# Columns' t2 as a unit-matrix matmul in steps 0 to 69 of the first image pair, and a new place in PSUM for the columns' n, u and input part

## The chip, the cores and the metric

The kernel runs on one core of one Trainium2 chip. The metric is the device time of one execution in microseconds. Engines are named as in the profile: PE is TensorE, DVE is VectorE, ACT is ScalarE, POOL is GpSimd, SP is SyncE, which issues most DMAs.

## What is computed

Eight images of 192 channels and 128 x 128 pixels are group-normalized. Each goes through four scans of a gated recurrent unit, along the rows in both directions and along the columns in both directions. The four results are averaged and added to the input.

```python
def step(h, xg):                       # xg = seq @ W_ih.T + b_ih, seq = x @ Wi.T + bi
    hg = h @ W_hh.T + b_hh
    r = sigmoid(xr + hr)
    z = sigmoid(xz + hz)
    n = tanh(xn + r * hn)
    return (1.0 - z) * n + z * h       # 64 wide, 128 steps
out = hs @ Wo.T + bo                   # back to 192 channels
x + (right + down + left + up) / 4.0
```

## The kernel before, in words

**Tiling.** Images are worked on in four pairs, g = 0 to 3. The two images of a pair fill the two halves of the 128 partitions with 64 hidden channels each. Two recurrences run side by side in each of the 128 steps t of a pair: c = 0 is the rows' scan, c = 1 the columns' scan. Each has 256 columns, two directions of 128 sequences.

**One step.** For each c there is this chain. PE adds the state part of gate r to the input part that it computed earlier (`h_r` after `x_r`), ACT makes r (`gate_r`), and DVE makes t1 = (hn + bias) * r (`make_t1`, line 994) and t2 = t1 + xn (`make_t2`, line 999). ACT makes n = tanh(t2) (`gate_n`, line 670), DVE u = (z - 1) * n (`make_u`, line 1004) and h = v - u (`make_h`, line 1013), where POOL has made v = z * h (`make_v`). The new h starts the next step's `h_r`. Each engine has one order for both chains. ACT: r rows, z rows, r columns, n rows, z columns, n columns. DVE: t1 rows, t2 rows, t1 columns, u rows, t2 columns, h rows, u columns, h columns, with other work at fixed places between them.

**PE and its quarters.** A product of 64 x 64 weights with 256 columns of fp32 is one matmul in the program and shows as two MATMUL rows, two passes, in the trace. The state parts (`h_part`, lines 860 and 861) work from each half of the partitions into the same half. The input parts (`x_part`, lines 840 and 842) work from each half into the other half. They use different quarters of the array and run beside each other. In a step PE's order is: h_r rows, x_r columns, h_n rows, x_n columns, h_z rows, x_z columns, h_r columns, h_n columns, then x_r, h_z columns, x_n and x_z, where these x parts are the rows' for step t + 1.

**Other work in the steps.** For pairs 1 to 3, the previous pair's output is finished in 96 units. The first 63 (in steps 3 to 65) each have two matmul pairs that fetch x (`unit_x_half`, lines 806 and 808, `beside_state` in `scan`) around h_n of the columns, two output products later (`unit_half`), and ACT's `add_bias`. The other units, in steps 73 to 124, have only the output products, and DVE adds x (`add_x`, line 1025). In pairs 0 to 2, steps 71 to 126 project the next pair's input in 32 tiles. A tile has two halves in quarters of the input parts around h_n of the columns (`project_high`, lines 756 and 758), two in quarters of the state parts (`project_straight`), and two again in quarters of the input parts (`project_crossed`, lines 781 and 783). The crossed ones stand in the next step around h_n of the columns, or, in eight steps of a pair, at the end of the same step; ACT then copies the tile out (`project_next`, line 650). In steps 0 to 63 of pairs 0 to 2 DVE also takes statistics for the next pair (line 986).

**PSUM.** `rx_ps` (bank 0 rows, bank 3 columns) holds r's input and, in its second half, xn. `hn_ps` (bank 1, bank 4) holds hn, then n, and u in its second half. `z_ps` (bank 2, bank 5) uses its first half only.

Of the kernel before, what the change touches and what calls it, by code (L numbers as in the profile page):

```python
# [5 lines left out]
def gru_scan_2d_kernel(nc: bass.Bass, x, wi_t, bi, w_ih_t, w_hh_t, b_ih, b_hh, wo_t, bo,  # L6
# [24 lines left out]
    T = WW  # L31
# [98 lines left out]
    with ctx:  # L130
# [73 lines left out]
        rx_ps = [bank[0], bank[3]]  # L204
        hn_ps = [bank[1], bank[4]]
        z_ps = [bank[2], bank[5]]
        fin_ps = [bank[0:3], bank[3:6]]
        proj_ps = bank[6:8]
        next_ps = bank[6]
# [56 lines left out]

        NSD = 16
        NSP = 3

        def state_before(g, t):  # L270

            return (T + 1) * g + t + 1
# [318 lines left out]
        def _(act):  # L591
# [75 lines left out]

            def gate_n(g, t, c):
                act.wait_ge(t2_ready[c], T * g + t + 1)
                act.activation(hn_ps[c][:, 0:N2], r[:, c, :], ACT.Tanh, bias=bih[:, 2:3]).then_inc(n_ready[c], 1)  # L670

            def scan(g):
                for t in range(T):
# [32 lines left out]
        def _(pe):  # L706
# [130 lines left out]
            def x_part(ps, gate, c, t, start):  # L837

                px = pair_of(seq, c, t)
                pe.matmul(as_pair(ps[LOW, :], c), wx[HIGH, gate, :], px[HIGH], start=start, stop=False,  # L840
                          skip_group_check=True)
                return pe.matmul(as_pair(ps[HIGH, :], c), wx[LOW, gate, :], px[LOW], start=start, stop=False,  # L842
                                 skip_group_check=True)

            def x_z(g, t, c):
                if T * g + t > 0:
                    pe.wait_ge(z_ready[c], T * g + t)
                x_part(z_ps[c][:, 0:N2], 1, c, t, True).then_inc(x_z_ready[c], 1)

            def x_r(g, t, c):  # L850
                if T * g + t > 0:
                    pe.wait_ge(t2_ready[c], T * g + t)
                x_part(rx_ps[c][:, 0:N2], 0, c, t, True)

            def x_n(g, t, c):
                x_part(rx_ps[c][:, N2:2 * N2], 2, c, t, False).then_inc(x_rn_ready[c], 1)

            def h_part(ps, gate, t, c, start):
                state = h[:, c, (t + 1) % 2, :]
# [8 lines left out]
                h_part(rx_ps[c], 0, t, c, False).then_inc(pre_r[c], 1)  # L868

            def h_n(g, t, c):  # L870
                h_part(hn_ps[c], 2, t, c, True).then_inc(pre_n[c], 1)

            def h_z(g, t, c):
                pe.wait_ge(x_z_ready[c], T * g + t + 1)
# [2 lines left out]
            def scan(g):  # L877
                if g == 0:
                    pe.wait_ge(seq_written, TILES)
                    pe.wait_ge(ident_loaded, 32)  # L880
                else:
                    pe.wait_ge(seq_fetched, 16 * PIECES * g)
                    for i in (1, 2):
                        pe.wait_ge(border_fetched[i], 16 * g)
                x_r(g, 0, 0)
                x_n(g, 0, 0)
                x_z(g, 0, 0)
                for t in range(T):
                    u = unit_at[t] if g > 0 and t in unit_at else None
                    m = project_at[t] if g + 1 < PAIRS and t in project_at else None  # L890

                    ends = project_ends[t] if g + 1 < PAIRS and t in project_ends and m is None else None
                    beside_state = u is not None and u < N_ACT
                    beside_input = u is not None and m is None

                    h_r(g, t, 0)
                    if g > 0 and t == 0:
                        for i in (0, 3):
                            pe.wait_ge(border_fetched[i], 16 * g)
                    x_r(g, t, 1)  # L900
                    h_n(g, t, 0)
                    x_n(g, t, 1)
                    h_z(g, t, 0)
                    x_z(g, t, 1)

                    h_r(g, t, 1)
                    if m is not None:
                        project_high(g + 1, m, 0)
                    if ends is not None:
                        project_crossed(g + 1, ends, 0)  # L910
                    if beside_state:
                        unit_x_half(g, u, 0)
                    h_n(g, t, 1)
                    if m is not None:
                        project_high(g + 1, m, 1)
                    if ends is not None:
                        project_crossed(g + 1, ends, 1)
                    if beside_state:
                        unit_x_half(g, u, 1)
                    if t + 1 < T:  # L920
                        x_r(g, t + 1, 0)
                    h_z(g, t, 1)
                    if t + 1 < T:
                        x_n(g, t + 1, 0)
                    if m is not None:
                        project_straight(g + 1, m, 0)
                    if beside_input:
                        unit_half(g, u, 0)
                    if t + 1 < T:
                        x_z(g, t + 1, 0)  # L930
                    if m is not None:
                        project_straight(g + 1, m, 1)
                    if beside_input:
                        unit_half(g, u, 1)
                    if u is not None and not beside_input:
                        for side in range(2):
                            unit_half(g, u, side)
                    if m is not None and t in project_ends:
                        for side in range(2):
                            project_crossed(g + 1, m, side)  # L940
                    if g + 1 < PAIRS:
                        if t == S_MEANS:
                            group_means(g + 1)
                        if t == S_CHANNELS:
                            channel_stats(g + 1)
                        if t == S_BIAS:
                            mean_bias(g + 1)
# [25 lines left out]
        def _(dve):  # L973
# [22 lines left out]

            def make_t2(g, t, c):
                dve.wait_ge(t1_ready[c], T * g + t + 1)
                dve.tensor_tensor(r[:, c, :], rx_ps[c][:, N2:2 * N2], r[:, c, :], ALU.add).then_inc(t2_ready[c], 1)  # L999

            def make_u(g, t, c):

                dve.wait_ge(n_ready[c], T * g + t + 1)
                dve.scalar_tensor_tensor(out=hn_ps[c][:, N2:2 * N2], in0=z[:, c, :], scalar=1.0, in1=hn_ps[c][:, 0:N2],  # L1004
                                         op0=ALU.subtract, op1=ALU.mult).then_inc(u_ready[c], 1)

            def make_h(g, t, c):
                k = T * g + t
                dve.wait_ge(u_ready[c], k + 1)
                dve.wait_ge(v_ready[c], k + 1)  # L1010
                if k >= 2:
                    dve.wait_ge(h_added[c], k - 1)
                dve.tensor_tensor(h[:, c, t % 2, :], v[:, c, :], hn_ps[c][:, N2:2 * N2], ALU.subtract)\  # L1013
                   .then_inc(h_ready[c], 1)

            def add_x(g, u, k):
# [13 lines left out]
            def scan(g):  # L1030
# [4 lines left out]
                for t in range(T):  # L1035
# [9 lines left out]
                        add_x(g, unit_at[t - 1], 1)  # L1045
                    make_t1(g, t, 1)
                    make_u(g, t, 0)
                    make_t2(g, t, 1)
                    make_h(g, t, 0)
                    if stats:  # L1050
                        half_chunk_stats(g + 1, t, 1)
# [171 lines left out]
```

## Time and profile before

| | before |
|---|---|
| median of 3 runs | 2473.11 us (2460.13 to 2480.77) |
| the profiled execution's own time | 2473.35 us |
| its span, first to last instruction | 2471.5 us |
| mean granted PE clock | 0.987 of full speed |
| busy share PE, DVE, ACT, POOL | 88%, 82%, 64%, 62% |
| line 840, 842, 860, 861: MATMUL rows each | 6144 of about 385 ns, pipelined, up to four at once |

All stretches of steps look alike, so one step of a kind shows its stage. In a timeline an instruction's end is its start plus its duration. A MATMUL row's end is modelled, so the starts are what is read from PE's rows.

### The profile page before, as it was taken

Reading aid. Unit: us, or ns where it says so; the run is one execution under the profiler, and the core shown is the slowest. Engines: PE = TensorE matmul, PEld = TensorE weight load, DVE = VectorE, ACT = ScalarE, POOL = GpSimd, SP = SyncE. Lnnn points to the kernel's source line nnn. Section 1 sums busy time; section 2 is a strip of 40 time slices with the busy share of each in tenths; the row PEclk is TensorE's granted clock in tenths of the full one; section 3 lists DMA queues with packets and bytes.
Section 4 is the critical chain, followed back from the end, with each engine's and each line's share of the span. In section 5 each row is a group of like instructions: output and inputs, shape, how many; then the busy total and the mean of one; then the engine's idle time right before and its main releaser. Section 6 shows DMA issues by size and latency. Waiting matters only on the chain.

```text
span 2471.5 us, 79952 instructions
## 1 busy us (share of the span) xinstructions
PE 2180.6 (88%) x31528; PEld 1412.0 (57%) x31528; DVE 2017.6 (82%) x4978; ACT 1569.6 (64%) x3390; POOL 1537.0 (62%) x2119
## 2 busy tenths in 40 slices
PE   0679999899979999999979999999979999999995
PEld 0345555566646666566546666565646666555574
DVE  7319999877769999887869999887867887888874
ACT  0126666677758887676657788676657888666600
POOL 2007777677767776666757677666766777777710
PEclk9999999999989999999999999999999999999998
DMA  9993332257789997789999998589986665334699
GB/s 353 292 229 102 97 98 72 87 148 217 235 241 245 249 247 188 184 220 271 302 280 237 237 253 209 156 223 272 307 261 170 155 148 133 74 96 95 157 328 372
DMA packets 325716, 509.19 MB, mean 206 GB/s; under 512 B 24928, under 2 KB 140000, under 8 KB 325344
## 3 DMA queue, kind: packets, MB, share of 16 engines
q1 hardware_dynamic: 307296, 478.23, 70.3%
q10 hardware_dynamic: 18048, 25.85, 3.0%
q8 instruction: 252, 4.13, 0.7%
q14 instruction: 120, 0.98, 0.1%
HBM read 352.98 MB, written 151.01 MB: 204 GB/s over the span
## 4 chain that ended last, share of the span: by engine, by line
DVE 33%; PE 31%; ACT 16%; issue 8%; DMA 6%; POOL 3%; SPq 1%; ACTq 0%; DVEq 0%; POOLq 0%
PE bank L860 19%; DVE r L994 12%; DVE r L999 11%; ACT r L662 7%; DVE h L1013 5%; ACT z L666 5%; DMA work<-x 4%; DVE bank L1004 3%; ACT bank L670 3%; PE bank L840 3%; PE bank L958 2%; PE bank L842 2%; ACT work L657 2%; PE bank L861 1%; DVE bn L986 1%
## 5 line engine op out<-in xcount | busy, mean ns | idle before, releaser
L860 PE MATMUL bank<-h,wh 64*64 64x256 f32 x6144 | 1496.5, 386 | 117.0 <-DVE h L1013 101.2
L840 PE MATMUL bank<-seq,wx 64*64 64x256 f32 x6144 | 1547.0, 384 | 32.4 <-DMA seq<-seq_next 22.1
L842 PE MATMUL bank<-seq,wx 64*64 64x256 f32 x6144 | 1547.7, 384 | 0.5 <-issue 0.5
L861 PE MATMUL bank<-h,wh 64*64 64x256 f32 x6144 | 1497.6, 386 | 0.4 <-issue 0.4
L546 POOL TENSOR_TENSOR v<-z,h 128x256 f32<-128x256 f32 x1024 | 747.6, 730 | 623.5 <-ACT z L666 597.8
L860 PEld LDWEIGHTS bank<-h,wh 64*64 64x64 f32 x6144 | 712.1, 133 | 584.2 <-DVE h L1013 416.7
L840 PEld LDWEIGHTS bank<-seq,wx 64*64 64x64 f32 x6144 | 753.9, 132 | 211.1 <-DVE r L999 105.8
L554 POOL TENSOR_TENSOR hsum<-hsum,h 128x256 f32<-128x256 f32 x1024 | 752.0, 734 | 128.7 <-DVE h L1013 109.4
L842 PEld LDWEIGHTS bank<-seq,wx 64*64 64x64 f32 x6144 | 751.3, 132 | 32.0 <-issue 3.1
L994 DVE SCALAR_TENSOR_TENSOR r<-bank,bhh,r 128x256 f32<-128x256 f32 x1024 | 490.1, 479 | 266.8 <-ACT r L662 230.2
L861 PEld LDWEIGHTS bank<-h,wh 64*64 64x64 f32 x6144 | 701.7, 133 | 1.0
L666 ACT ACTIVATE z<-bank,brz 128x256 f32<-128x256 f32 x1024 | 486.0, 475 | 312.0 <-PE bank L861 293.6
L662 ACT ACTIVATE r<-bank,brz 128x256 f32<-128x256 f32 x1024 | 485.7, 474 | 184.2 <-PE bank L861 183.9
L670 ACT ACTIVATE bank<-r,bih 128x256 f32<-128x256 f32 x1024 | 486.0, 475 | 115.3 <-DVE r L999 103.3
L1004 DVE SCALAR_TENSOR_TENSOR bank<-z,bank 128x256 f32<-128x256 f32 x1024 | 430.7, 421 | 68.2 <-ACT bank L670 67.5
L1013 DVE TENSOR_TENSOR h<-v,bank 128x256 f32<-128x256 f32 x1024 | 425.4, 415 | 24.8 <-issue 4.0
L999 DVE TENSOR_TENSOR r<-bank,r 128x256 f32<-128x256 f32 x1024 | 430.9, 421 | 17.7
L986 DVE BATCH_NORM_STATS2 bn<-work 128x6 f32<-128x384 f32 x384 | 211.8, 551 | 6.7 <-DMA work<-x 6.7
L824 PE MATMUL bank<-work,wo_a 64*64 64x256 f32 x768 | 205.3, 384 | 1.2 <-issue 1.2
L826 PE MATMUL bank<-work,wo_b 64*64 64x256 f32 x768 | 205.8, 385 | 0.0
L808 PE MATMUL bank<-work,ident 64*64 64x256 f32 x756 | 203.0, 389 | 0.0
L806 PE MATMUL bank<-work,ident 64*64 64x256 f32 x756 | 197.5, 381 | 0.0
(94 smaller groups left out, 2436.8 us busy)
## 6 DMA issues: line engine op xcount, KB each, us to landing
work<-x SPq DMA_DIRECT2D x384, 384.0 KB, 6.2
out<-work SPq DMA_DIRECT2D x192, 384.0 KB, 4.7
work<-x SPq DMA_DIRECT2D x143, 512.0 KB, 7.0
work<-x SPq DMA_DIRECT2D x286, 128.0 KB, 7.2
work<-x SPq DMA_DIRECT2D x32, 768.0 KB, 6.7
seq_next<-work SPq DMA_DIRECT2D x48, 512.0 KB, 6.9
work<-hsum_last SPq DMA_DIRECT2D x48, 512.0 KB, 7.1
seq<-x SPq DMA_DIRECT2D x17, 512.0 KB, 7.1
```

The lines of the kernel that those rows point to most:

```text
L546: pool.tensor_tensor(v[:, c, :], z[:, c, :], h[:, c, (t + 1) % 2, :], ALU.mult).then_inc(v_ready[c], 1)
L554: pool.tensor_tensor(px, px, as_pair(h[:, c, t % 2, :], c), ALU.add).then_inc(h_added[c], 1)
L662: act.activation(r[:, c, :], rx_ps[c][:, 0:N2], ACT.Sigmoid, bias=brz[:, 0:1]).then_inc(r_ready[c], 1)
L666: act.activation(z[:, c, :], z_ps[c][:, 0:N2], ACT.Sigmoid, bias=brz[:, 1:2]).then_inc(z_ready[c], 1)
L670: act.activation(hn_ps[c][:, 0:N2], r[:, c, :], ACT.Tanh, bias=bih[:, 2:3]).then_inc(n_ready[c], 1)
L840: pe.matmul(as_pair(ps[LOW, :], c), wx[HIGH, gate, :], px[HIGH], start=start, stop=False, skip_group_check=True)
L842: return pe.matmul(as_pair(ps[HIGH, :], c), wx[LOW, gate, :], px[LOW], start=start, stop=False, skip_group_check=True)
L860: pe.matmul(ps[LOW, 0:N2], wh[LOW, gate, :], state[LOW], start=start, stop=True, skip_group_check=True)
L861: return pe.matmul(ps[HIGH, 0:N2], wh[HIGH, gate, :], state[HIGH], start=start, stop=True, skip_group_check=True)
L994: dve.scalar_tensor_tensor(out=r[:, c, :], in0=hn_ps[c][:, 0:N2], scalar=bhh[:, 2:3], in1=r[:, c, :], op0=ALU.add, op1=ALU.mult).then_inc( ...
L999: dve.tensor_tensor(r[:, c, :], rx_ps[c][:, N2:2 * N2], r[:, c, :], ALU.add).then_inc(t2_ready[c], 1)
L1013: dve.tensor_tensor(h[:, c, t % 2, :], v[:, c, :], hn_ps[c][:, N2:2 * N2], ALU.subtract)\
```

## The change

In the columns' chain, n and u move into the free second half of `z_ps` (bank 5), and the input part of n moves from the second half of `rx_ps` (bank 3) into the second half of `hn_ps` (bank 4), beside the state part of n. The waits follow. The columns' x_z now waits for the columns' h as well, and so stands behind h_r of the columns and not ahead of it; x_n of the columns waits for n of the step before; x_r of the columns waits for r and not for t2. This holds in all 512 steps. In steps 0 to 69 of pair 0, t2 of the columns is no DVE addition: PE adds t1 to xn in PSUM with a 64 x 64 unit matrix (`add_t1`, in the quarters of the state parts), and n reads PSUM.

```diff
+        xn_ps = [rx_ps[0][:, N2:2 * N2], hn_ps[1][:, N2:2 * N2]]
+        n_ps = [hn_ps[0][:, 0:N2], z_ps[1][:, N2:2 * N2]]
+        u_ps = [hn_ps[0][:, N2:2 * N2], z_ps[1][:, N2:2 * N2]]
...
+        def t2_on_pe(g, t):
+            return g == 0 and t < PROJECT_FROM - 1
...
             def gate_n(g, t, c):
                 act.wait_ge(t2_ready[c], T * g + t + 1)
-                act.activation(hn_ps[c][:, 0:N2], r[:, c, :], ACT.Tanh, bias=bih[:, 2:3]).then_inc(n_ready[c], 1)
+                before = xn_ps[1] if c == 1 and t2_on_pe(g, t) else r[:, c, :]
+                act.activation(n_ps[c], before, ACT.Tanh, bias=bih[:, 2:3]).then_inc(n_ready[c], 1)
...
             def x_z(g, t, c):
                 if T * g + t > 0:
                     pe.wait_ge(z_ready[c], T * g + t)
+                if c == 1 and t > 0:
+                    pe.wait_ge(h_ready[1], state_before(g, t))
...
             def x_r(g, t, c):
                 if T * g + t > 0:
-                    pe.wait_ge(t2_ready[c], T * g + t)
+                    pe.wait_ge(t2_ready[0] if c == 0 else r_ready[1], T * g + t)
...
             def x_n(g, t, c):
-                x_part(rx_ps[c][:, N2:2 * N2], 2, c, t, False).then_inc(x_rn_ready[c], 1)
+                if c == 1 and T * g + t > 0:
+                    pe.wait_ge(n_ready[1], T * g + t)
+                x_part(xn_ps[c], 2, c, t, c == 1).then_inc(x_rn_ready[c], 1)
...
+            def add_t1(g, t):
+                pe.wait_ge(t1_ready[1], T * g + t + 1)
+                pe.matmul(xn_ps[1][LOW], ident[LOW, :], r[LOW, 1, :], start=False, stop=True, skip_group_check=True)
+                pe.matmul(xn_ps[1][HIGH], ident[HIGH, :], r[HIGH, 1, :], start=False, stop=True,
+                          skip_group_check=True).then_inc(t2_ready[1], 1)
...
                     h_z(g, t, 0)
+
+                    h_r(g, t, 1)
                     x_z(g, t, 1)
-
-                    h_r(g, t, 1)
...
+                    if t2_on_pe(g, t):
+                        add_t1(g, t)
                     if t + 1 < T:
                         x_z(g, t + 1, 0)
...
-                    make_t2(g, t, 1)
+                    if not t2_on_pe(g, t):
+                        make_t2(g, t, 1)
```

The first place is PE's order in a step with a unit (pair 2, before): bank 2 is h_z of the rows, bank 5 x_z of the columns and later their h_z, bank 3 h_r, bank 4 h_n, and bank 7 the two halves that fetch x.

```order
L860 MATMUL bank2<-h,wh 64x256 [waits x_z_ready0]
L861 MATMUL bank2<-h,wh 64x256
L840 MATMUL bank5<-seq,wx 64x256 [waits z_ready1]
L842 MATMUL bank5<-seq,wx 64x256
L860 MATMUL bank3<-h,wh 64x256 [waits x_rn_ready1,h_ready1]
L861 MATMUL bank3<-h,wh 64x256
L806 MATMUL bank7<-work,ident 64x4x64 [waits unit_finished,xf_loaded2,unit_added,hs_loaded0]
L808 MATMUL bank7<-work,ident 64x4x64
L860 MATMUL bank4<-h,wh 64x256
L861 MATMUL bank4<-h,wh 64x256
L806 MATMUL bank7<-work,ident 64x4x64 [waits xf_loaded2]
L808 MATMUL bank7<-work,ident 64x4x64
```

The same place in the changed program:

```order
L872 MATMUL bank2<-h,wh 64x256 [waits x_z_ready0]
L873 MATMUL bank2<-h,wh 64x256
L872 MATMUL bank3<-h,wh 64x256 [waits x_rn_ready1,h_ready1]
L873 MATMUL bank3<-h,wh 64x256
L848 MATMUL bank5<-seq,wx 64x256 [waits h_ready1,z_ready1]
L850 MATMUL bank5<-seq,wx 64x256
L814 MATMUL bank7<-work,ident 64x4x64 [waits unit_finished,xf_loaded2,unit_added,hs_loaded0]
L816 MATMUL bank7<-work,ident 64x4x64
L872 MATMUL bank4<-h,wh 64x256
L873 MATMUL bank4<-h,wh 64x256
L814 MATMUL bank7<-work,ident 64x4x64 [waits xf_loaded2]
L816 MATMUL bank7<-work,ident 64x4x64
```

The input part x_z moved from ahead of h_r (bank 3) to behind it, between h_r and the first fetch of x, and it has two waits where it had one.

The second place is the end of a step of pair 0 on PE, before. Bank 5 is h_z of the columns; banks 0 and 2 are x_n and x_z of the rows for the next step, then its h_r.

```order
L860 MATMUL bank5<-h,wh 64x256 [waits x_z_ready1]
L861 MATMUL bank5<-h,wh 64x256
L840 MATMUL bank0<-seq,wx 64x256
L842 MATMUL bank0<-seq,wx 64x256
L840 MATMUL bank2<-seq,wx 64x256 [waits z_ready0]
L842 MATMUL bank2<-seq,wx 64x256
L860 MATMUL bank0<-h,wh 64x256 [waits x_rn_ready0,h_ready0]
```

The same place in the changed program:

```order
L872 MATMUL bank5<-h,wh 64x256 [waits x_z_ready1]
L873 MATMUL bank5<-h,wh 64x256
L848 MATMUL bank0<-seq,wx 64x256
L850 MATMUL bank0<-seq,wx 64x256
L888 MATMUL bank4<-r,ident 64x256 [waits t1_ready1]
L889 MATMUL bank4<-r,ident 64x256
L848 MATMUL bank2<-seq,wx 64x256 [waits z_ready0]
L850 MATMUL bank2<-seq,wx 64x256
L872 MATMUL bank0<-h,wh 64x256 [waits x_rn_ready0,h_ready0]
```

The unit-matrix pair into bank 4 came in between x_n and x_z of the rows, with its wait for t1.

The third place is DVE's order in a step of pair 0, before, from t1 of the columns (994) over u of the rows (1004), t2 of the columns (999) and h of the rows (1013) to h of the columns.

```order
L994 SCALAR_TENSOR_TENSOR r<-bank,bhh,r 128x256 [waits pre_n1,r_ready1]
L1004 SCALAR_TENSOR_TENSOR bank<-z,bank 128x256 [waits n_ready0]
L999 TENSOR_TENSOR r<-bank,r 128x256 [waits t1_ready1]
L1013 TENSOR_TENSOR h<-v,bank 128x256 [waits h_added0,v_ready0,u_ready0]
L986 BN_STATS bn<-work 128x6
L1004 SCALAR_TENSOR_TENSOR bank<-z,bank 128x256 [waits n_ready1]
L1013 TENSOR_TENSOR h<-v,bank 128x256 [waits h_added1,v_ready1,u_ready1]
```

The same place in the changed program:

```order
L1015 SCALAR_TENSOR_TENSOR r<-bank,bhh,r 128x256 [waits pre_n1,r_ready1]
L1025 SCALAR_TENSOR_TENSOR bank<-z,bank 128x256 [waits n_ready0]
L1034 TENSOR_TENSOR h<-v,bank 128x256 [waits h_added0,v_ready0,u_ready0]
L1007 BN_STATS bn<-work 128x6
L1025 SCALAR_TENSOR_TENSOR bank<-z,bank 128x256 [waits n_ready1]
L1034 TENSOR_TENSOR h<-v,bank 128x256 [waits h_added1,v_ready1,u_ready1]
```

The addition between u and h of the rows is gone from DVE.

## Rows read from the trace of the kernel before

**Rows 1.** The page: engines, and the chain that ended last by engine.
```profile
PE 2180.6 (88%) x31528; PEld 1412.0 (57%) x31528; DVE 2017.6 (82%) x4978; ACT 1569.6 (64%) x3390; POOL 1537.0 (62%) x2119
...
DVE 33%; PE 31%; ACT 16%; issue 8%; DMA 6%; POOL 3%; SPq 1%; ACTq 0%; DVEq 0%; POOLq 0%
```

**Rows 2.** Timeline of DVE, pair 0 step 43: start, duration, engine, line, operation.
```profile
348.58 0.41 DVE L1013 TENSOR_TENSOR h<-v,bank 128x256 f32<-128x256 f32 x1
...
349.38 0.41 DVE L1004 SCALAR_TENSOR_TENSOR bank<-z,bank 128x256 f32<-128x256 f32 x1
349.83 0.42 DVE L1013 TENSOR_TENSOR h<-v,bank 128x256 f32<-128x256 f32 x1
350.25 0.48 DVE L994 SCALAR_TENSOR_TENSOR r<-bank,bhh,r 128x256 f32<-128x256 f32 x1
...
351.58 0.47 DVE L994 SCALAR_TENSOR_TENSOR r<-bank,bhh,r 128x256 f32<-128x256 f32 x1
351.97 0.42 DVE L1004 SCALAR_TENSOR_TENSOR bank<-z,bank 128x256 f32<-128x256 f32 x1
352.29 0.42 DVE L999 TENSOR_TENSOR r<-bank,r 128x256 f32<-128x256 f32 x1
352.63 0.41 DVE L1013 TENSOR_TENSOR h<-v,bank 128x256 f32<-128x256 f32 x1
```

**Rows 3.** Timeline of ACT, the same step.
```profile
349.74 0.47 ACT L662 ACTIVATE r<-bank,brz 128x256 f32<-128x256 f32 x1 [0.56 <-PE bank L861]
...
351.04 0.47 ACT L662 ACTIVATE r<-bank,brz 128x256 f32<-128x256 f32 x1
351.41 0.47 ACT L670 ACTIVATE bank<-r,bih 128x256 f32<-128x256 f32 x1
```

**Rows 4.** Timeline of PE, the same step: h_r of rows (first pass), of columns (second).
```profile
349.05 0.43 PE L860 MATMUL bank<-h,wh 64*64 64x256 f32 x1 [0.32 <-DVE h L1013]
...
350.62 0.38 PE L861 MATMUL bank<-h,wh 64*64 64x256 f32 x1
```

**Rows 5.** Timeline of PE, pair 1 step 32, a unit's fetches of x.
```profile
851.22 0.40 PE L806 MATMUL bank<-work,ident 64*64 64x256 f32 x1
...
851.50 0.38 PE L808 MATMUL bank<-work,ident 64*64 64x256 f32 x1
...
851.93 0.38 PE L808 MATMUL bank<-work,ident 64*64 64x256 f32 x1
```

**Rows 6.** Timeline of DVE, pair 1 step 32.
```profile
849.33 0.41 DVE L1013 TENSOR_TENSOR h<-v,bank 128x256 f32<-128x256 f32 x1
...
852.33 0.47 DVE L994 SCALAR_TENSOR_TENSOR r<-bank,bhh,r 128x256 f32<-128x256 f32 x1
...
853.38 0.41 DVE L1013 TENSOR_TENSOR h<-v,bank 128x256 f32<-128x256 f32 x1
```

**Rows 7.** Timeline of PE, pair 3 step 32: second passes of h_z columns and x_r.
```profile
1967.74 0.38 PE L861 MATMUL bank<-h,wh 64*64 64x256 f32 x1
...
1967.93 0.37 PE L840 MATMUL bank<-seq,wx 64*64 64x256 f32 x1
```

**Rows 8.** Timeline of ACT, the same step: z of the columns.
```profile
1968.39 0.47 ACT L666 ACTIVATE z<-bank,brz 128x256 f32<-128x256 f32 x1 [0.30 <-PE bank L861]
```

**Rows 9.** Timeline of DVE, the same step: h of rows before, t1 of columns.
```profile
1964.78 0.41 DVE L1013 TENSOR_TENSOR h<-v,bank 128x256 f32<-128x256 f32 x1
...
1967.75 0.48 DVE L994 SCALAR_TENSOR_TENSOR r<-bank,bhh,r 128x256 f32<-128x256 f32 x1 [0.35 <-ACT r L662]
```

**Rows 10.** Timeline of PE, pair 1 step 104: h_n of the columns, second pass.
```profile
1159.58 0.38 PE L861 MATMUL bank<-h,wh 64*64 64x256 f32 x1
```

**Rows 11.** Timeline of DVE, the same step: t1 of the columns, which waits for PE.
```profile
1160.08 0.48 DVE L994 SCALAR_TENSOR_TENSOR r<-bank,bhh,r 128x256 f32<-128x256 f32 x1 [3.30 <-PE bank L861]
```

**Rows 12.** Timeline of ACT after pair 0 step 78, which projects a whole tile.
```profile
501.30 0.69 ACT L650 ACTIVATE work<-bank,bseq 128x512 f32<-128x512 f32 x1 [0.92 <-PE bank L783]
```

**Rows 13.** Groups by line and form: the halves of add_x on DVE.
```profile
L1025 DVE SCALAR_TENSOR_TENSOR work<-bank,bo_unit,work 128x256 f32<-128x256 f32 x132 | 62.8, 476 | 0.0
```

More of the change, by code:

```diff
@@ L870, in h_n @@
             def h_n(g, t, c):
-                h_part(hn_ps[c], 2, t, c, True).then_inc(pre_n[c], 1)
+                h_part(hn_ps[c], 2, t, c, c == 0).then_inc(pre_n[c], 1)
+            def add_t1(g, t):
[3 more added lines that the diff above has]
+                          skip_group_check=True).then_inc(t2_ready[1], 1)
             def h_z(g, t, c):
@@ L998, in make_t2 @@
                 dve.wait_ge(t1_ready[c], T * g + t + 1)
-                dve.tensor_tensor(r[:, c, :], rx_ps[c][:, N2:2 * N2], r[:, c, :], ALU.add).then_inc(t2_ready[c], 1)
+                dve.tensor_tensor(r[:, c, :], xn_ps[c], r[:, c, :], ALU.add).then_inc(t2_ready[c], 1)
             def make_u(g, t, c):
                 dve.wait_ge(n_ready[c], T * g + t + 1)
-                dve.scalar_tensor_tensor(out=hn_ps[c][:, N2:2 * N2], in0=z[:, c, :], scalar=1.0, in1=hn_ps[c][:, 0:N2],
+                dve.scalar_tensor_tensor(out=u_ps[c], in0=z[:, c, :], scalar=1.0, in1=n_ps[c],
                                          op0=ALU.subtract, op1=ALU.mult).then_inc(u_ready[c], 1)
@@ L1012, in make_h @@
                     dve.wait_ge(h_added[c], k - 1)
-                dve.tensor_tensor(h[:, c, t % 2, :], v[:, c, :], hn_ps[c][:, N2:2 * N2], ALU.subtract)\
+                dve.tensor_tensor(h[:, c, t % 2, :], v[:, c, :], u_ps[c], ALU.subtract)\
                    .then_inc(h_ready[c], 1)
```

## The prediction

> **What bounds the kernel now.** I read the page first. No engine is full: PE is busy for 88% of the span, DVE 82%, ACT 64%, and the chain that ended last changes between DVE, PE and ACT all the time [rows 1]. So a loop of dependences from step to step sets the pace, and the question is which one. The timelines of single steps show it.
>
> In pair 0 the rows' h of step 42 ends at 348.58 + 0.41 = 348.99 and that of step 43 at 352.63 + 0.41 = 353.04 [rows 2]: 4.05 us a step. The way between them: PE begins the rows' h_r 0.06 later, at 349.05, and runs without a gap to the columns' h_r, whose second pass begins at 350.62 [rows 4]. The columns' r starts at 351.04, 0.42 after that pass. ACT's order puts the rows' n behind it, at 351.41, 0.10 before r ends [rows 3]. DVE then works back to back: t1 of the columns at 351.58, u of the rows at 351.97, t2 of the columns at 352.29, h of the rows at 352.63 [rows 2]. Two things follow. The columns' t2 stands between u and h of the rows and costs the loop time. And each delay of the columns' t1 moves u, t2 and h of the rows one for one.
>
> With units the way is the same: in pair 1 the columns' t1 starts at 852.33 and the rows' h 1.05 later, at 853.38 [rows 6]. In pair 3, without statistics, t1 stands at 1967.75, 2.56 after the end of h at 1964.78 + 0.41 = 1965.19 [rows 9]; in pair 1 it is 852.33 - 849.74 = 2.59.
>
> **The DVE addition taken away, pair 0, steps 1 to 63.** Rows' loop: u ends at 352.39; a dependent h starts 0.04 later, as the columns' do (349.38 + 0.41 = 349.79, then 349.83) [rows 2]. So h would begin at 352.43 instead of 352.63 and end at 352.84, and this loop takes 4.05 - 0.20 = 3.85.
>
> Columns' loop, from the start of r: r 0.47; 0.04 to DVE (349.74 + 0.47 = 350.21, t1 of the rows at 350.25); t1 0.47; 0.06 to PE. The added pair of matmuls is two passes in each of two quarters, as h_r is. From the first pass of h_r (349.05) to ACT's r (349.74) it is 0.69 [rows 3, 4], which I take; n then starts 1.73 after r did. n takes 0.47, 0.04 and u 0.41, 0.04 and h 0.42, 0.06 and h_r 0.69 until the next r: 3.86. That is 0.01 above the rows' loop, so both are about as long, and the step takes 3.87. The gain is 0.18 x 63 = 11 us. Bounds: if the matmul costs no more than the DVE addition did, the rows' loop alone decides, 0.20 x 69 = 14 us; if it costs 0.18 more than 0.69, nothing is gained. For steps 64 to 69, which hold long statistics, I count nothing. PE's x_z of the rows stands behind add_t1's wait; it is needed only by h_z of the next step. ACT reading PSUM in n is priced at nothing: r, which reads PSUM, takes 0.47, as n does [rows 3].
>
> **x_z of the columns behind h_r, all steps.** In plain steps (pair 0 to step 70, pair 3 from step 66) the quarters of the input parts stand idle beside h_r and h_n of the columns, and the move is free: that idle slot is its cover. With a unit, or while a tile is projected, the cover is gone. The fetch of x began at 851.22, its second pass at 851.50 and the second fetch's at 851.93 [rows 5]. x_z now takes the first place, the first fetch the second, and so on: the first fetch's second pass begins at 851.93 instead of 851.50, one slot of 0.43 later.
>
> Who waits for that? h_n of the columns stands behind this fetch in the program. A row shows what that does. h_z of the columns stands behind x_r in the program; its second pass began first, at 1967.74, against 1967.93 for x_r's [rows 7]. Yet z started at 1968.39 [rows 8]: 0.65 after its own second pass, 0.46 after x_r's, where r needed 0.42. So matmuls in other quarters may start early, but their ends are reported in program order. h_n's end will then be reported behind the fetch's, and t1 waits for it. Where t1 waited for h_n alone, it began 1160.08 - 1159.58 = 0.50 after the second pass [rows 10, 11]; with the 0.04 by which z was late beyond r's 0.42 I take 0.53. So t1 begins at 851.93 + 0.53 = 852.46 instead of 852.33. Relative to the end of h that is 2.72, against 2.59 and 2.56 now.
>
> The Trainium skill, "TensorE: Matmul & The Clock Gate", section "What overlaps and what doesn't", says that matmuls start and end strictly in program order. The trace agrees on the ends and not on the starts. By the rule taken whole, h_n would also start behind the fetch, and the sum would be near 2670, by the rows 2517.
>
> DVE's back-to-back overlap with the statistics ahead of t1 goes too, so I take 0.145 a step in 122 steps with units and statistics (steps 3 to 63, pairs 1 and 2) and 0.16 in 65 without (63 of pair 3, step 64 of pairs 1 and 2): 18 + 10 = 28 us. Bounds: 0 if h_n's end is not held; 0.26 a step if x_z's second wait puts it 0.1 later than the fetch stands now.
>
> The three pairs that project have 56 such steps each, 168 in all, with a half tile between h_r and h_n. In 136 I take 0.16, 22 us. In 32 steps of pairs 1 and 2 a half of add_x, 0.476 [rows 13], already holds DVE up; between 0 and 0.16 I take 0.08, 2.5 us. Eight steps of a pair run a whole tile through as one serial chain, and ACT stood idle 0.92 for its end before copying it, with r of the rows behind [rows 12]. This chain is pushed by up to the slot of 0.43; I take 0.35, which is 0.2 more than counted: 24 x 0.2 = 5 us. Less some 2 us where PE waits for a tile's load anyway, this is 27.
>
> New waits: x_n of the columns waits for n of the step before. n ends about 0.2 after the rows' h, 0.4 in pair 0 with add_t1 (2.20 after r, against 352.84 - 351.04 = 1.80 for the rows' h); x_n's turn on PE comes 0.5 after h. I count nothing; if it were later by 0.1, what stands behind it (h_z of the rows, h_r of the columns) would move by as much. x_r's wait becomes earlier. No DMA is moved.
>
> **Sum.** 2473.35 (the profiled execution, 1.85 above its span, and 0.2 above the median of 2473.11) - 11 + 28 + 27 = 2517, 1.8% slower.
>
> **Rivals.**
> 1. Not slower: h_n's end isn't held by the fetch. This decides from one number, t1's start with units: at 2.6 after h or below, the 28 us and most of the 27 fall away. Only the serial tiles remain, 24 x 0.35 = 8 us, and with the 11 gained it is 2471. For it: the case seen is x_r and h_z [rows 7, 8], not fetch and h_n. Against it: the two cases have the same form.
> 2. Starts are held in program order too: another slot of 0.43 in 355 steps, 153 us, 2670. Against it: the starts [rows 7]. This is the rule of the Trainium skill, "TensorE: Matmul & The Clock Gate", named above.
> 3. The added matmul or x_z's dispatch costs more: no gain in pair 0, or 0.1 more in 355 steps; 2528 to 2555.
>
> The change does what it says: the order shows 70 additions gone and 70 pairs added.
>
> **How the numbers follow.** My forecast has a chance of 0.73, with a range of its own of 2497 to 2545. Rival 1 has 0.15 (2463 to 2480), rival 2 0.03, rival 3 beyond that range 0.06, and 0.03 is for a gain that I don't see. To hold 8 in 10 the range must reach rival 1's middle: 2470 to 2545. A measurement of this kernel tells about 1%, 25 us, from no change. Slower than 2498 is 0.80, within 1% 0.17, faster 0.03.
>
> **What would show it.** Right: in the profile after, pair 0's plain steps take 3.85 to 3.9; with units they take 4.19; t1 of the columns waits for PE in them, 0.5 after the fetch's second pass. Wrong: steps with units stay at 4.05, or pair 0's stay there too because n is late.

## The result, and the profile after

The changed kernel takes 2520.61 us (median of 4 runs, 2512.93 to 2524.03) against 2469.2 us for the kernel before (4 runs, 2460.13 to 2480.77, three of them those of the table ahead): a ratio of 1.0197, 95% interval 1.0171 to 1.0223. It is slower by about 2%; 2517 had been forecast.

The page of the changed kernel, its count of instructions, its engines and the chain that ended last by engine, stands against [rows 1]:

```profile
span 2511.1 us, 80950 instructions
...
PE 2294.4 (91%) x31808; PEld 1581.0 (63%) x31808; DVE 2018.3 (80%) x4908; ACT 1548.4 (62%) x3390; POOL 1533.5 (61%) x2119
...
PE 66%; DVE 12%; DMA 6%; ACT 5%; issue 5%; POOL 4%; ACTq 1%; SPq 0%; POOLq 0%; DVEq 0%
```

The chain now runs mainly through PE (66%, before 31%) and hardly through DVE (12%, before 33%). PE has only 280 more rows of 31528, so this isn't added work: the engines now wait for PE's ends where they waited for DVE's before.

**Pair 0, step 43.** Timeline of DVE after (h is line 1034, t1 1015, u 1025; compare [rows 2]):

```profile
338.52 0.42 DVE L1034 TENSOR_TENSOR h<-v,bank 128x256 f32<-128x256 f32 x1
...
341.53 0.48 DVE L1015 SCALAR_TENSOR_TENSOR r<-bank,bhh,r 128x256 f32<-128x256 f32 x1
341.93 0.42 DVE L1025 SCALAR_TENSOR_TENSOR bank<-z,bank 128x256 f32<-128x256 f32 x1
342.39 0.42 DVE L1034 TENSOR_TENSOR h<-v,bank 128x256 f32<-128x256 f32 x1
```

Between u and h nothing stands any more: h begins 0.46 us after u, where it was 0.66. From h to h it is 342.39 - 338.52 = 3.87 us; it was 4.05. The added matmuls on PE (lines 888 and 889), and n of the columns on ACT (line 678), which waits for them:

```profile
342.07 0.43 PE L888 MATMUL bank<-r,ident 64*64 64x256 f32 x1
...
342.35 0.38 PE L889 MATMUL bank<-r,ident 64*64 64x256 f32 x1
```

```profile
342.77 0.45 ACT L678 ACTIVATE bank<-bank,bih 128x256 f32<-128x256 f32 x1 [0.35 <-PE bank L889]
```

PE begins 0.06 after t1 ends (341.53 + 0.48 = 342.01) and ACT 0.70 after that.

**Pair 3, step 32, a step with a unit.** Timeline of PE after, columns: x_z (line 848), the first fetch (lines 816 and 814) and h_n (line 873). Two rows of one line here are its two passes.

```profile
2002.85 0.40 PE L848 MATMUL bank<-seq,wx 64*64 64x256 f32 x1
...
2003.31 0.38 PE L816 MATMUL bank<-work,ident 64*64 64x256 f32 x1
2003.34 0.38 PE L814 MATMUL bank<-work,ident 64*64 64x256 f32 x1
...
2003.43 0.38 PE L873 MATMUL bank<-h,wh 64*64 64x256 f32 x1
...
2003.56 0.38 PE L814 MATMUL bank<-work,ident 64*64 64x256 f32 x1
```

Timeline of DVE in the same step: h of the rows, t1 of the columns, the next h (compare [rows 9]):

```profile
2000.96 0.41 DVE L1034 TENSOR_TENSOR h<-v,bank 128x256 f32<-128x256 f32 x1
...
2004.10 0.48 DVE L1015 SCALAR_TENSOR_TENSOR r<-bank,bhh,r 128x256 f32<-128x256 f32 x1 [0.50 <-PE bank L873]
...
2005.16 0.41 DVE L1034 TENSOR_TENSOR h<-v,bank 128x256 f32<-128x256 f32 x1
```

h_n's second pass began at 2003.43. t1 began 0.67 later, but 0.54 after the fetch's second pass at 2003.56. Relative to the end of h (2000.96 + 0.41 = 2001.37), t1 stands at 2.73 instead of 2.56. The step takes 4.20.

**Where the time went.** I added up stretches of steps, from the end of one rows' h to that of a later one, in the profiled execution of each kernel; units are steps 0 to 64 of pairs 1 to 3, projection is steps 71 to 127 of pairs 0 to 2. Three more columns are experiments told of below.

| us | before | after | no second wait | both mended | pair 0 alone |
|---|---|---|---|---|---|
| pair 0, steps 0 to 64 | 258.96 | 247.46 | 247.32 | 247.27 | 247.28 |
| units | 789.79 | 818.59 | 798.96 | 791.59 | 791.05 |
| projection | 725.11 | 751.51 | 737.52 | 733.86 | 724.85 |

The change brings -11.5, +28.8 and +26.4. The sum is +43.7. The two profiled executions differ by 39.6, since the first h came 2.5 us earlier after, the end was 2.6 us shorter, and the other steps took 1.0 more. These parts vary from run to run (the first h came 172 to 181 us after the start in the ten profiled executions). The medians differ by 51.4, more than the stretches explain: the profiled execution of the changed kernel was the fastest of its four.

### The profile page after: what moved, and what is told of

The parts are those of the page before. It is cut to its first block, busy times and chain, and to the rows that moved or that the text cites. A ratio compares the mean times of both kernels' runs of the same rounds, so it can differ in the third digit from the quotient of the medians.

```text
span 2511.1 us, 80950 instructions
## 1 busy us (share of the span) xinstructions
PE 2294.4 (91%) x31808; PEld 1581.0 (63%) x31808; DVE 2018.3 (80%) x4908; ACT 1548.4 (62%) x3390; POOL 1533.5 (61%) x2119
## 3 DMA queue, kind: packets, MB, share of 16 engines
q8 instruction: 256, 4.19, 0.7%
## 4 chain that ended last, share of the span: by engine, by line
PE 66%; DVE 12%; DMA 6%; ACT 5%; issue 5%; POOL 4%; ACTq 1%; SPq 0%; POOLq 0%; DVEq 0%
PE bank L872 30%; PE bank L848 13%; PE bank L850 5%; DMA work<-x 4%; DVE r L1015 4%; PE bank L816 3%; PE bank L873 3%; PE bank L832 2%; ACT z L673 2%; DVE r L1020 2%; DVE bank L1025 2%; ACT r L669 2%; DVE h L1034 2%; PE bank L766 1%; POOL v L553 1%
## 5 line engine op out<-in xcount | busy, mean ns | idle before, releaser
L848 PE MATMUL bank<-seq,wx 64*64 64x256 f32 x6144 | 1631.0, 385 | 30.1 <-DMA seq<-seq_next 21.5
L850 PE MATMUL bank<-seq,wx 64*64 64x256 f32 x6144 | 1640.2, 387 | 0.0
L872 PE MATMUL bank<-h,wh 64*64 64x256 f32 x6144 | 1533.0, 386 | 49.7 <-DVE h L1034 36.1
L873 PE MATMUL bank<-h,wh 64*64 64x256 f32 x6144 | 1534.4, 386 | 1.2 <-issue 1.1
L872 PEld LDWEIGHTS bank<-h,wh 64*64 64x64 f32 x6144 | 703.1, 132 | 501.7 <-DVE h L1034 343.0
L848 PEld LDWEIGHTS bank<-seq,wx 64*64 64x64 f32 x6144 | 716.6, 132 | 155.2 <-DVE r L1020 52.5
L850 PEld LDWEIGHTS bank<-seq,wx 64*64 64x64 f32 x6144 | 716.7, 132 | 5.9 <-issue 1.0
L873 PEld LDWEIGHTS bank<-h,wh 64*64 64x64 f32 x6144 | 696.0, 132 | 6.5 <-issue 0.7
L678 ACT ACTIVATE bank<-r,bih 128x256 f32<-128x256 f32 x954 | 452.7, 475 | 39.5 <-DVE r L1020 38.4
L1020 DVE TENSOR_TENSOR r<-bank,r 128x256 f32<-128x256 f32 x954 | 402.2, 422 | 17.7
L816 PE MATMUL bank<-work,ident 64*64 64x256 f32 x756 | 193.5, 376 | 0.0
L814 PE MATMUL bank<-work,ident 64*64 64x256 f32 x756 | 193.4, 376 | 0.0
```

The source lines that it names most:

```text
L678: act.activation(n_ps[c], before, ACT.Tanh, bias=bih[:, 2:3]).then_inc(n_ready[c], 1)
L872: pe.matmul(ps[LOW, 0:N2], wh[LOW, gate, :], state[LOW], start=start, stop=True, skip_group_check=True)
L873: return pe.matmul(ps[HIGH, 0:N2], wh[HIGH, gate, :], state[HIGH], start=start, stop=True, skip_group_check=True)
```

## The experiments

My theory was that x_z behind h_r pushes the fetch, and that h_n's end, hence t1, is held behind the fetch because ends come in program order. The first rival was that the new PSUM places and waits cost the time. The second was that fuller quarters do, whatever the program order.

**h_n of the columns last, in the kernel before.** No quarter gets more work; only h_n's place in the program is later.

```diff
-                    h_n(g, t, 1)
                     if m is not None:
                         project_high(g + 1, m, 1)
                     if ends is not None:
                         project_crossed(g + 1, ends, 1)
                     if beside_state:
                         unit_x_half(g, u, 1)
+                    h_n(g, t, 1)
```

> The kernel before with h_n of the columns written behind both halves of the fetch (and of the half tiles), x_z and all else as before. No quarter gets more work and none gets its work in another order; only the place of h_n in the program is later. In the kernel before the second half of the fetch begins its second pass where the first half does in the changed kernel. If ends are held in program order, t1 of the columns begins about 2.72 us after the rows' h in steps with units although h_n itself runs as early as before, and about 0.16 us in each of 355 steps is lost: some 55 us, ratio 1.022. If ends are not held, h_n, which finds its quarters idle, ends as early as before, t1 stays at 2.59 and the ratio is 1.00.

Measured: 2525.98 us, ratio 1.0217 (1.0201 to 1.0233). Timeline of PE in pair 3, step 32: h_n's second pass (line 861), then the second fetch's (line 808). The timeline of DVE in that step stands below it: h of the rows and t1 of the columns.

```profile
2011.55 0.38 PE L861 MATMUL bank<-h,wh 64*64 64x256 f32 x1
...
2011.79 0.38 PE L808 MATMUL bank<-work,ident 64*64 64x256 f32 x1
```

```profile
2009.08 0.41 DVE L1013 TENSOR_TENSOR h<-v,bank 128x256 f32<-128x256 f32 x1
...
2012.34 0.48 DVE L994 SCALAR_TENSOR_TENSOR r<-bank,bhh,r 128x256 f32<-128x256 f32 x1 [0.64 <-PE bank L861]
```

h_n's second pass still begins 2011.55 - 2009.49 = 2.06 after h, as in all these kernels, yet t1 begins 0.79 after it and 0.55 after the second fetch's pass. The trace also has the moment at which h_n's semaphore was raised, relative to h (medians of steps 5 to 62): 2.46 in all pairs of the kernel before; here 2.63 in pair 1 and 2.74 in pairs 2 and 3, 0.45 behind the second fetch's second pass (2.18 and 2.30); in the changed kernel 2.63 in pairs 1 to 3, 0.44 behind the first fetch's (2.19). So h_n's end is held by what stands ahead of it in the program, with nothing else changed. That settles the mechanism. The total came out as expected, though not its parts: t1 stood at 2.74 with units in pair 1 and at 2.85 in pairs 2 and 3, where the fetch is later (see the next experiment), and the units lost 41 us, where they lose 29 in the changed kernel; the projection lost only 8, where it loses 26 there.

**x_z of the columns behind h_r, in the kernel before, and nothing else.**

```diff
                     h_z(g, t, 0)
-                    x_z(g, t, 1)
 
                     h_r(g, t, 1)
+                    x_z(g, t, 1)
```

> The kernel before with one line moved: x_z of the columns behind h_r of the columns, in all steps. No matmul is added, no PSUM place and no wait is changed; t2 of the columns stays on DVE everywhere. If the move itself is the cause (x_z takes the first place behind h_r, the fetch or the half tile moves one slot back, and the end of h_n is held behind it), t1 of the columns begins about 2.72 us after the rows' h ends in steps with units, against 2.59 before, these steps take about 4.19 instead of 4.05, and the run is about 55 us longer than before: some 2528, ratio 1.022. Pair 0 keeps 4.05 in its plain steps. If the new PSUM places and the waits that come with them are the cause, this kernel takes what before takes: ratio 1.00, t1 at 2.59.

Measured: 2488.87 us, ratio 1.0067 (1.0045 to 1.0089). Neither expectation held: some 17 us of the 55. In steps with units t1 stood at 2.617 after h, not at 2.73, and the steps took 4.09. x_z's first pass began 1.37 after h, not 1.48 as in the changed kernel. So in pair 1 the move itself puts the fetch's second pass back by 0.32 (in step 32 from 1.75 to 2.07 after h), not by 0.43. In the kernel before, with x_z elsewhere, the fetch began 1.48 after h in pair 1 (851.22 in [rows 5], h's end at 849.74). x_z alone can begin 0.11 earlier than that, but in the changed kernel it doesn't. The difference at x_z between the two kernels is a wait.

In pairs 2 and 3 the move costs the fetch only 0.21. Timeline of PE in the kernel before, pair 3 step 32 (h's end at 1965.19, [rows 9]): the first fetch's first and second pass, and h_n's second.

```profile
1966.78 0.40 PE L806 MATMUL bank<-work,ident 64*64 64x256 f32 x1
...
1967.06 0.38 PE L808 MATMUL bank<-work,ident 64*64 64x256 f32 x1
...
1967.25 0.38 PE L861 MATMUL bank<-h,wh 64*64 64x256 f32 x1
```

The fetch begins at 1.59 and not at 1.48, and its second pass at 1.86 (median) and not at 1.75. What the program has there in pairs 2 and 3 and not in pair 1 is one wait more ahead of the fetch, for `unit_finished`, which counts the units that DVE finished in the scans before and was fulfilled before this pair's scan began. No run takes this wait away, so that it is the cause is argued and not shown. With x_z ahead of the fetch this difference is gone: its second pass stands at 2.07 in all three pairs, and at 2.19 in the changed kernel.

**The changed kernel without that wait.** In it x_z of the columns waits for z and for h. h_r, ahead of it on the same queue, has waited for the same h, so the second wait is always fulfilled when it comes up.

```diff
             def x_z(g, t, c):
                 if T * g + t > 0:
                     pe.wait_ge(z_ready[c], T * g + t)
-                if c == 1 and t > 0:
-                    pe.wait_ge(h_ready[1], state_before(g, t))
```

> The changed kernel without the new wait of the columns' x_z on the columns' h of the step before; h_r of the columns, which now stands ahead of x_z on the same queue, waits for the same h, so the order of the data is unchanged. x_z stays behind h_r, all else stays. If this second wait is what makes the move dear (with it x_z's first pass began 1.48 us after the rows' h, without it, in the kernel with the move alone, 1.37), the fetch's second pass returns from 2.18 to 2.07, t1 of the columns from 2.73 to 2.62, steps with units from 4.20 to 4.10, and with the gain of 11.5 us in pair 0 the run takes about 11 us less than the kernel with the move alone: 2478, ratio to before 1.000 to 1.004. If the new PSUM places or the other new waits are the cause, t1 stays at 2.73 and the run at 2515 to 2520, ratio 1.02.

Measured: 2479.27 us (10 runs), ratio 1.0036 (1.0021 to 1.0051), as expected. The page counts 508 instructions fewer than that of the changed kernel, 4 x 127 steps:

```profile
span 2482.6 us, 80442 instructions
```

Timeline of PE in pair 3, step 32: x_z's first pass (line 848), h_n's second (line 871), the first fetch's second (line 814); below it DVE's h of the rows and t1 of the columns.

```profile
1975.37 0.43 PE L848 MATMUL bank<-seq,wx 64*64 64x256 f32 x1
...
1976.06 0.38 PE L871 MATMUL bank<-h,wh 64*64 64x256 f32 x1
1976.07 0.38 PE L814 MATMUL bank<-work,ident 64*64 64x256 f32 x1
```

```profile
1973.59 0.41 DVE L1032 TENSOR_TENSOR h<-v,bank 128x256 f32<-128x256 f32 x1
...
1976.62 0.48 DVE L1013 SCALAR_TENSOR_TENSOR r<-bank,bhh,r 128x256 f32<-128x256 f32 x1 [0.38 <-ACT r L669]
```

With h's end at 1974.00, x_z begins at 1.37 (it was 1.48) and the fetch's second pass at 2.07 (2.19), nearly together with h_n's at 2.06. t1 begins at 2.62 and is 0.55 behind the fetch again. A wait that never waits thus cost some 34 to 40 us, 19.6 + 14.0 by the table's stretches and (1.0197 - 1.0036) x 2470 = 40 by the ratios, as an instruction of its own on PE's queue ahead of a matmul on whose end others hang. It is the same 0.11 as at the fetch of pairs 2 and 3 in the kernel before. The new PSUM places and the other new waits are all still in this kernel, yet with units its t1 (2.62) and its period (4.09) are those of the kernel with the move alone, which has none of them: there they cost nothing. The Trainium skill, "Perfetto Trace Analysis", section "Identifying Dependency Chains", says that an instruction that waits on several engines may get separate semaphore instructions ahead of it for the further conditions; the count of 508 agrees.

**h_n ahead of the fetch, in the changed kernel.** x_z, its wait and the late fetch stay.

```diff
                     x_z(g, t, 1)
+                    h_n(g, t, 1)
                     if m is not None:
                         project_high(g + 1, m, 0)
...
                         unit_x_half(g, u, 0)
-                    h_n(g, t, 1)
```

> The changed kernel with h_n of the columns written ahead of the first half of the fetch, of the half tile and of the crossed tile; x_z of the columns stays behind h_r of the columns, so the fetch still begins one slot later. If a matmul's end is held behind the ends of what stands ahead of it in program order, h_n is free now: t1 of the columns returns to 2.56 to 2.62 us after the rows' h in steps with units, their period to 4.05, and the gain of 11 us in pair 0 remains: 2460 to 2480, ratio to before 0.995 to 1.003. What may stay are some microseconds of the tiles that run through in one step. If the full quarters (the slot itself, contention of input parts with state parts) are the cause, t1 stays at 2.72 and the run near 2517, ratio 1.02.

Measured: 2494.27 us, ratio 1.0084 (1.0063 to 1.0104), between the two expectations. In pair 3 the theory holds: t1 follows h_n, not the fetch. DVE in step 32, h of the rows and t1 of the columns, and PE's second pass of h_n (line 873):

```profile
1984.68 0.41 DVE L1034 TENSOR_TENSOR h<-v,bank 128x256 f32<-128x256 f32 x1
...
1987.65 0.48 DVE L1015 SCALAR_TENSOR_TENSOR r<-bank,bhh,r 128x256 f32<-128x256 f32 x1 [0.16 <-ACT r L669]
```

```profile
1987.15 0.38 PE L873 MATMUL bank<-h,wh 64*64 64x256 f32 x1
```

t1 stands at 2.56 after h, 0.50 behind h_n, and these steps take 4.03. In pairs 1 and 2 its median was 2.72 all the same. The timelines of ACT and DVE there (pair 1, the step behind the h at 901.77) show why: a unit's copy (line 664), r of the rows, then t1 and t2 of the rows, the statistics (line 1007), t1 of the columns.

```profile
902.50 0.69 ACT L664 ACTIVATE work<-bank,bo_high 128x512 f32<-128x512 f32 x1
903.08 0.47 ACT L669 ACTIVATE r<-bank,brz 128x256 f32<-128x256 f32 x1
```

```profile
901.77 0.41 DVE L1034 TENSOR_TENSOR h<-v,bank 128x256 f32<-128x256 f32 x1
...
903.58 0.48 DVE L1015 SCALAR_TENSOR_TENSOR r<-bank,bhh,r 128x256 f32<-128x256 f32 x1
904.10 0.42 DVE L1020 TENSOR_TENSOR r<-bank,r 128x256 f32<-128x256 f32 x1
904.44 0.55 DVE L1007 BATCH_NORM_STATS2 bn<-work 128x6 f32<-128x384 f32 x1
904.91 0.47 DVE L1015 SCALAR_TENSOR_TENSOR r<-bank,bhh,r 128x256 f32<-128x256 f32 x1
```

The late fetch pushes the rows' input parts that share its quarters, up to x_z, whose last pass on PE is this:

```profile
902.03 0.37 PE L850 MATMUL bank<-seq,wx 64*64 64x256 f32 x1
```

The second half of the unit's output products stands behind x_z in the program, and ACT's copy of the unit, which needs it, begins 0.47 after this pass. In step 32 of pair 1 that distance is 0.47 to 0.49 in this kernel, in the changed one and in the one without the second wait, where x_z comes earlier; in the kernel before it is 0.68, so there the copy waits for something else. The semaphores say the same (medians of pairs 1 to 3): the unit's is raised 0.06 after x_z's in every kernel, and the copy begins 0.02 after that in these three, 0.08 to 0.21 in the kernel before. Relative to h (901.77 + 0.41 = 902.18) the copy begins at 0.32 (median 0.30; 0.12 before) and r of the rows at 0.90 (0.75 before), and DVE runs back to back from there to t1 of the columns at 2.73. A late fetch has two ways to t1, and the longer one hid the other in the changed kernel. In pair 3, without statistics, DVE has room for it. Against the kernel before, the units lose 9.9 us here and the projection 20.0; in the projection t1 stood at 2.82 to 2.83 in pairs 1 and 2 (2.66 before), and what holds it there is not shown.

**Both mended:** the changed kernel without the second wait and with h_n ahead of the fetch.

> The changed kernel with both mended: no second wait at x_z of the columns, and h_n of the columns ahead of the fetch. If the end of h_n held behind the fetch and the late fetch (through ACT's copy of the unit, the rows' r, and DVE's order) are all there is, t1 stands at 2.56 in pair 3 and at 2.59 to 2.63 in steps with statistics, and the run is 3 to 12 us below the kernel without the second wait alone: 2464 to 2474, ratio 0.997 to 1.001. If h_n ahead of the fetch makes the fetch later and this costs as much as it saves, it equals the kernel without the second wait.

Measured: 2473.84 us (10 runs), ratio 1.0010 (0.9990 to 1.0029), the upper end of what was expected. t1 stands at 2.56 in pair 3 and at 2.63 to 2.64 in pairs 1 and 2 (2.59 to 2.63 expected). The steps with units cost 1.8 us more than before and the projection 8.8, about what pair 0 gains.

**The changed kernel with t2 on DVE everywhere.**

```diff
         def t2_on_pe(g, t):
 
-            return g == 0 and t < PROJECT_FROM - 1
+            return False
```

> The changed kernel without the added pair of matmuls: t2 of the columns is a DVE addition in all steps, also in steps 0 to 69 of the first pair; new PSUM places, waits and the place of x_z stay. If the added matmuls save what the first pair saves, its plain steps return to 4.05 us and the run is 11.5 us longer than the changed kernel: about 2532, ratio to before 1.024 to 1.025. If the new PSUM places alone shortened the first pair's steps, they stay at 3.87 and the run at 2520.

Measured: 2525.16 us, ratio 1.0213 (1.0197 to 1.0228), between the two expectations. The totals can't tell it from the changed kernel, their intervals overlap; the stretch can: pair 0's steps 0 to 64 took 258.97 us again, a step 4.05. So the added matmuls saved the 11.5 us, and not the new places, which also cost nothing there (258.96 before).

**The change in pair 0, steps 0 to 69, alone,** and the kernel before in all other steps.

```diff
+        def z_behind(g, t):
+            return t2_on_pe(g, t) or (t > 0 and t2_on_pe(g, t - 1))
...
-                    x_z(g, t, 1)
+                    if not z_behind(g, t):
+                        x_z(g, t, 1)
 
                     h_r(g, t, 1)
+                    if z_behind(g, t):
+                        x_z(g, t, 1)
```

> The change in pair 0, steps 0 to 69, alone: the new PSUM places, x_z of the columns behind h_r and t2 as matmuls in these steps only, everything as in the kernel before in all others. There the slot beside h_r and h_n of the columns is idle, so the gain of 11.5 us should remain and nothing be lost: 2458 to 2462 against 2471, ratio 0.9955, with pair 0's plain steps at 3.87 and steps with units at 4.05. If something else in the scan or its beginning lost time with the new places, the ratio is 1.00 or above.

Measured: 2459.88 us (12 runs), ratio 0.9958 (0.9943 to 0.9972). It beats both kernels, by the gain of pair 0 and nothing else (last column of the table).

**The same, and pair 3 from step 67 on too:**

```diff
-            return g == 0 and t < PROJECT_FROM - 1
+            return (g == 0 and t < PROJECT_FROM - 1) or (g == PAIRS - 1 and t > ACT_UNITS_UNTIL)
```

> As the kernel with the change in pair 0 alone, and the same in pair 3 from step 67 on, where no unit stands beside the columns' matmuls. 31 of these 61 steps hold nothing but the recurrence and took 4.13 us, 30 hold a unit on the input side and took 4.07. If DVE's addition between u and h of the rows costs the loop there what it cost in pair 0, 0.18 to 0.2 a step, 11 us more are gained: ratio 0.991. If what paces these steps is something else (their t1 stands at 2.66 instead of 2.56 in the plain ones), less than 4 us more: ratio 0.994 to 0.9955.

Measured: 2461.57 us (12 runs), ratio 0.9960 (0.9946 to 0.9975): no more gain, just above the second expectation. The steps divide otherwise than was written there: in the kernel before it is the 33 steps behind a unit that take 4.12, the others take 4.03 (medians). Timeline of PE from step 100 into 101 of pair 3: the added matmuls (line 900), the second half of a unit's output products (line 842), the next h_r of the rows (line 883); below it DVE's h of the rows from step 99 to 102.

```profile
2233.28 0.37 PE L900 MATMUL bank<-r,ident 64*64 64x256 f32 x1
...
2233.72 0.38 PE L842 MATMUL bank<-work,wo_c 64*64 64x256 f32 x1
...
2233.94 0.38 PE L842 MATMUL bank<-work,wo_c 64*64 64x256 f32 x1
...
2234.15 0.37 PE L883 MATMUL bank<-h,wh 64*64 64x256 f32 x1
```

```profile
2229.65 0.42 DVE L1049 TENSOR_TENSOR h<-v,bank 128x256 f32<-128x256 f32 x1
...
2233.51 0.42 DVE L1049 TENSOR_TENSOR h<-v,bank 128x256 f32<-128x256 f32 x1
...
2237.69 0.42 DVE L1049 TENSOR_TENSOR h<-v,bank 128x256 f32<-128x256 f32 x1
...
2241.98 0.42 DVE L1049 TENSOR_TENSOR h<-v,bank 128x256 f32<-128x256 f32 x1
```

Step 100 takes 3.86, as in pair 0. But the unit's second half stands behind the added matmuls and uses the same quarters, and h_r of the rows can begin only 0.22 after h (2233.93) instead of 0.06. Step 101 then takes 4.18 and step 102, behind a second unit in a row, 4.29; before, these three steps took 4.03, 4.11 and 4.12. Over steps 68 to 127 the 27 steps with no unit ahead gain 4.6 us and the 33 behind a unit lose 3.4. Over steps 71 to 127 pair 3 took 228.25 us, against 228.68 before.

## Why the prediction was right

- **DVE's addition gone from pair 0: held.** 3.867 a step over steps 1 to 63 (3.87 said), 11.5 us (11 said). From the added matmul's first pass to ACT it is 342.77 - 342.07 = 0.70, where 0.69 was taken from h_r and r. Steps 64 to 69, counted at nothing, brought nothing (+0.4 us over steps 64 to 71).
- **h_n's end held behind the fetch: held,** and shown alone by the kernel with h_n last. t1 at 2.729 (2.72 said), steps with units 4.20 (4.19 said), 28.8 us (28 said). That the 28 came out is in part luck: it was worked out from the fetch of pair 1 alone. In pairs 2 and 3 the fetch's second pass stood at 1.86 before; by the same rule, a slot of 0.43 and then 0.53, t1 would have gone to 2.82 there and the loss to 0.23 and 0.26 a step. It did not: behind x_z the fetch stands at the same place in all three pairs.
- **One slot of 0.43: the place was right, the reason for it only in part.** The fetch's second pass stands at 2.185 after h in all three pairs, where 851.93 - 849.74 = 2.19 was said; it moved by 0.43 in pair 1, but by 0.32 in pairs 2 and 3. But I took the whole 0.43 for x_z's two passes, because x_z would begin where the fetch had begun. Without its second wait it begins 0.11 earlier, since the quarters stand idle then, and the move costs 0.32 (0.21 in pairs 2 and 3). I had listed that wait as a bound on top of the 0.43; it was inside. This matters more than 0.11 of 0.43 suggests: before, the fetch's end had 0.27 to spare in pair 1 until it could hold t1 (1.75 + 0.54 = 2.29 against 2.56) and 0.16 in pairs 2 and 3, and the move alone just uses that up (2.07 + 0.54 = 2.61). So the wait made 34 to 40 us of the loss, and the kernel without it is at 1.0036.
- **The projection: held in its sum** (26.4 us, 27 said), not in all its parts. A step behind one that runs a whole tile through went from 4.79 to 5.18 in pair 0 (medians of 8), 0.39, where 0.35 was said; the others, from 4.03 to 4.20, 0.17, where 0.16 was said. In pairs 1 and 2 t1 stood at 2.66 already before (2.56 in pair 0, medians), and they lose less (+5.4 and +9.6 against +11.4 in pair 0).
- **The rival that ends are not held** would have shown t1 at 2.6 or below and 2471. Its time is what one gets by mending the order and the wait together (2473.84).
- **The rival that starts are held too** is excluded: h_n's second pass begins at 2.06 after h whatever stands ahead of it, also with two fetches there. The rule behind it, in the Trainium skill, "TensorE: Matmul & The Clock Gate", section "What overlaps and what doesn't", that matmuls start and end strictly in program order, agrees here for ends only.
- **The rival of a dearer added matmul** is excluded by the 0.70; the 0.1 of x_z's dispatch was paid, inside the slot.
- **What I didn't see** is the second way from the late fetch to t1, through the rows' x_z, ACT's copy, r of the rows and DVE's order. It changed no number of the forecast, since the way over h_n was longer, but it is why h_n's place alone gives back only part. The new waits of x_n and x_r, taken as nothing, cost nothing in steps with units and in pair 0, as the kernels without the second wait and with t2 on DVE show.

## What to carry to other kernels

When a matmul is moved in PE's program, look at what stands *behind* it in the program, not only at its quarter of the array: in these runs the engine that waited for a later, independent matmul was released only after the earlier ones had ended. So put the matmul on whose end an engine hangs ahead of those that nobody hurries for, and make no wait on PE's queue that an earlier wait on the same queue already covers. And use a new data layout only in the stages that gain by it: here the gain lay in 70 steps of 512 and the costs in the others.

## What the runs showed of the hardware

- Matmuls in other quarters overtook in their starts, but not in their reported ends: with two fetches ahead of it in the program, h_n's second pass began 0.24 before the last fetch's, and t1 waited 0.79 for it instead of 0.50. With h_n's second pass at 2.06 after h each time, its semaphore was raised at 2.46, 2.63 or 2.74, as the fetch ahead of it ended.
- A wait that is already fulfilled was not free on PE: one more of them put the matmuls behind it 0.11 us later at x_z (1.37 to 1.48 after h), and in the kernel before at the fetch of pairs 2 and 3 against pair 1 (1.48 to 1.59), where one wait more is the only difference found. Where the quarters were busy with x_z anyway, the fetch's extra wait cost nothing.
- A matmul whose input came late held those behind it in the same quarters: in pair 3 the added matmuls put the next step's h_r 0.16 us later behind a unit, and three quarters of what the other steps gained was lost there.
